# Feed-forward products on two halves of the array, own block per iteration, and small reciprocals, in a fused attention and feed-forward kernel

## The reference

```python
xn = _layernorm(x)
q, k, v = xn @ wq + bq, xn @ wk + bk, xn @ wv + bv      # 16 query heads, 2 key/value heads of 16
q, k = rotated(q) * hd ** (-0.5), rotated(k)            # sin/cos tables over the 1024 positions
attn = softmax(einsum('bqhd,bkhd->bhqk', q, k_exp) * hd ** (-0.5))
a = einsum('bhqk,bkhd->bqhd', attn, v_exp).reshape(b, s, d) @ wo + bo
hidden = fwht(silu(xn @ W1.T) * (xn @ W3.T))            # 1024 wide, Walsh-Hadamard transform
out = x + a + hidden @ W2.T
```

## Time and profile before

| | us |
|---|---|
| median of 3 runs | 1303.58 |
| lowest and highest | 1293.02, 1316.16 |
| the profiled execution | 1307.79 |
| its span, first to last instruction | 1305.6 |
| mean granted clock of TensorE | 0.904 of 2.4 GHz |
| busy: PE, DVE, ACT, POOL | 1125.1, 827.6, 711.4, 351.6 |

### The profile page before, as it was taken

One profiled execution on the slowest core, in us unless ns is written; L12 is line 12 of the kernel. 1 busy time (PEld: TensorE's weight loads), 2 busy tenths in 40 slices (PEclk: granted clock), 3 DMA queues, 4 the chain that ended last, 5 costly groups with the idle time before them and its releaser, 6 DMA issues.

```text
span 1305.6 us, 16047 instructions
## 1 busy us (share of the span) xinstructions
PE 1125.1 (86%) x6048; PEld 538.3 (41%) x6048; DVE 827.6 (63%) x860; ACT 711.4 (54%) x1320; POOL 351.6 (27%) x300
## 2 busy tenths in 40 slices
PE   2276899978998899988998899978998999998985
PEld 1243454543444444443444434444444344533322
DVE  3766547666676657667676767667766667656611
ACT  2123347654674557654774557655774467544561
POOL 1836503205241053305241053105330013100000
PEclk9698899988998989999998999989999699977675
DMA  6330012000120022100120022000200011000001
GB/s 201 102 106 1 3 62 84 22 20 20 54 76 22 23 93 69 36 19 23 56 73 21 24 94 84 21 22 25 70 22 26 10 41 46 21 21 9 9 9 41
DMA packets 44796, 58.08 MB, mean 44 GB/s; under 512 B 11184, under 2 KB 26416, under 8 KB 44720
## 3 DMA queue, kind: packets, MB, share of 16 engines
q1 hardware_dynamic: 41408, 52.34, 13.7%
q10 hardware_dynamic: 3312, 4.72, 1.0%
HBM read 33.95 MB, written 13.63 MB: 36 GB/s over the span
## 4 chain that ended last, share of the span: by engine, by line
PE 73%; DVE 15%; issue 6%; POOL 2%; ACT 2%; ACTq 1%; SPq 0%; DMA 0%; POOLq 0%
PE ps L963 27%; PE ps L983 14%; PE ps L1067 14%; PE ps L1054 14%; DVE negpart L832 8%; PE ps L993 3%; DVE recips L863 2%; DVE y L869 1%; DVE y L814 1%; DVE stats L788 1%; PE ps L999 1%; DVE mturned L858 1%; ACTq L648 1%; DVE xnt L799 1%; DVE mturned L856 1%
## 5 line engine op out<-in xcount | busy, mean ns | idle before, releaser
L832 DVE TENSOR_REDUCE negpart<-ps 128x2 f32<-128x1024 f32 x512 | 626.5, 1225 | 388.8 <-PE ps L983 388.1
L709 ACT ACTIVATE work<-ps 128x512 f32<-128x512 f32 x1024 | 553.2, 598 | 396.1 <-PE ps L1054 391.0
L983 PE MATMUL ps<-kb,qh 48*128 48x512 f32 x1024 | 253.6, 480 | 106.5 <-DVE negpart L832 28.7
L1067 PE MATMUL ps<-work,vb 128*32 128x512 f32 x2048 | 301.3, 663 | 1.3 <-ACT work L709 1.2
L1054 PE MATMUL ps<-qh,kb 50*128 50x512 f32 x1024 | 271.9, 493 | 11.2 <-ACT work L709 11.2
L983 PEld LDWEIGHTS ps<-kb,qh 48*128 48x128 f32 x1024 | 105.8, 199 | 323.9 <-issue 139.7
L963 PE MATMUL ps<-xnt,w_p 128*128 128x512 f32 x768 | 218.4, 421 | 10.5 <-DVE negpart L832 6.5
L1054 PEld LDWEIGHTS ps<-qh,kb 50*128 50x128 f32 x1024 | 112.1, 200 | 147.5 <-issue 67.8
L963 PEld LDWEIGHTS ps<-xnt,w_p 128*128 128x128 f32 x768 | 138.3, 193 | 82.6 <-issue 49.9
L585 POOL TENSOR_TENSOR hid_p<-hid,hid_p 128x512 fp32r<-128x512 f32 x64 | 83.3, 1302 | 203.0 <-ACT hid_p L700 203.0
L581 POOL TENSOR_TENSOR hid<-hid 128x512 f32<-128x512 f32 x64 | 82.3, 1286 | 188.4 <-ACT hid L696 188.4
(11 more groups left out here) (104 smaller groups left out, 458.4 us busy)
## 6 DMA issues: line engine op xcount, KB each, us to landing
qh<-qk_parts SPq DMA_DIRECT2D x192, 64.0 KB, 2.1
y<-in_x SPq DMA_DIRECT2D x8, 512.0 KB, 4.2
recips<-osum SPq DMA_DIRECT2D x128, 32.0 KB, 2.0
attnt<-osum SPq DMA_DIRECT2D x128, 32.0 KB, 2.0
out<-y SPq DMA_DIRECT2D x8, 512.0 KB, 2.8
xn<-in_x SPq DMA_DIRECT2D x7, 512.0 KB, 3.9
qk_parts<-qe SPq DMA_DIRECT2D x14, 256.0 KB, 2.4
qk_parts<-xn SPq DMA_DIRECT2D x14, 256.0 KB, 2.4
```

Source lines behind the costliest of these rows:

```text
L709: nc.scalar.activation(prob[j % 2][:, h, :], ps[:, 4 + u % 3, :], ACT.Exp, scale=SCALE).then_inc(exp_done, 1)
L832: nc.vector.tensor_reduce(negpart[a][:, f, :, h, t, e], two(slot), AX.X, ALU.max, negate=True).then_inc(ring_free[slot], 1)
L983: m = pe.matmul(bank[:, r, :], qh[2 * q + f][rows, h, t * P:(t + 1) * P], kb[i % 2][rows, e * 512:(e + 1) * 512], start=True, stop=True)
L1067: m = pe.matmul(ps[VW * h:VW * (h + 1), 7, :], vb[b % 2][g][:, kt, :], prob[j % 2][:, h, :], start=(kt == 0), stop=(kt == ST - 1))
```

## The change

- UP: rows 0 to 63 of the array hold `W1`'s weights and rows 64 to 127 `W3`'s. The 256 input rows are taken in four parts of 64 (`KC`), so a chunk has 24 matmuls of 64 rows, in 12 pairs that write two banks. The tokens have to stand in both halves of the partitions: SP writes the turned tokens (`xt`) to DRAM (`store_turned`) and reads them back twice (`load_turned`) into `xf`.
- DN: 48 matmuls of 64 rows, in 24 pairs; each half sums into a bank of its own, and VectorE adds both (`down`).
- UP and DN of block i stand in iteration i, for all 8 iterations. In the opening stand 24 S1 alone.
- The row of tokens gives way to an order for each kind of period. A kind with `x` is one in which an MT or a VT stands too. ScalarE's and VectorE's orders have kinds too.
- The reciprocals are taken of one copy of each sum, 128 x 32 numbers, through DRAM (`turn_sums`, `spread_recips`), and spread to 128 x 512 by eight transfers.
- The statistics of block i + 3 are taken at p = 8 to 12, one tile each, not together after p = 13, and its normalisation at p = 13 and 14.
- `mturned` has one buffer for each half instead of two; `recips` one instead of two.

```diff
@@ main_entry @@
-        return ("WO", i - 1, p - 2) if i > 0 else ("DN", 0, p - 2)
-    if 4 <= p < 12 and i + 1 < NBLK:
-        return ("UP", i + 1, p - 4)
-    if p >= 12 and i + 1 < NBLK:
-        return ("DN", i + 1, p - 12)
+        return ("WO", i - 1, p - 2) if i > 0 else ("W2", p - 2)
+    if 4 <= p < 12:
+        return ("UP", i, p - 4)
+    if p >= 12:
+        return ("DN", i, p - 12)
@@ walk_iteration @@
+        if kind == "UP":
+            own(0, 1)
+            first(1)
+            scores(0)
+            extra()
+            sums_before()
+            scores(1)
+            first(1)
+            own(2, 3)
+            first(1)
+            scores(2)
+            sums(i, 2 * p)
+            scores(3)
+            first(1)
...
+        elif kind == "XT":
+            sums_before()
+            own(0)
+            first(1)
+            extra()
+            first(1)
+            scores(0)
+            own(1)
+            scores(1)
...
@@ move_sums, on SP @@
-                for h in range(QUAD):
-                    to = (a * QUAD + h) * HD
-                    sp.dma_start(recips[to:to + HD, f, :], osum[VW * h + HD:VW * (h + 1), :]).then_inc(moved[f], 16)
+                sp.dma_start(sums_rows[f, a * QUAD:(a + 1) * QUAD, :], osum[HD:P:VW, :]).then_inc(sums_out[f], 16)
...
+            def turn_sums(i, f):
+                sp.wait_ge(sums_out[f], 32 * (i + 1))
...
+                sp.dma_start(dens[f][:, :], sums_rows[f].rearrange("h (g n) -> (h g) n", g=HD)).then_inc(dens_in[f], 16)
+
+            def spread_recips(i, f):
+                sp.wait_ge(recip_done[f], i + 1)
...
+                sp.dma_start(recip_rows[f].rearrange("h (g n) -> (h g) n", g=HD), dens[f][:, :]).then_inc(recip_out[f], 16)
+                sp.wait_ge(recip_out[f], 16 * (i + 1))
+                for h in range(2 * QUAD):
+                    sp.dma_start(recips[HD * h:HD * (h + 1), :],
+                                 recip_rows[f, h].partition_broadcast(HD)).then_inc(recips_in, 16)
@@ down and reciprocals, on VectorE @@
-                nc.vector.tensor_tensor(at, at, two(slot)[:, 0, 0:D], ALU.add).then_inc(ring_free[slot], 1)
+                nc.vector.tensor_tensor(at, at, two(slot)[:, 0, 0:D], ALU.add).then_inc(down_half, 1)
+                dve.wait_ge(down_half, BT * m + t + 1)
+                nc.vector.tensor_tensor(at, at, two(slot)[:, 1, 0:D], ALU.add).then_inc(ring_free[slot], 1)
...
-                dve.wait_ge(moved[f], N_MOVE * 2 * (i + 1))
-                nc.vector.reciprocal(recips[:, f, :], recips[:, f, :]).then_inc(recip_done, 1)
+                dve.wait_ge(dens_in[f], 16 * (i + 1))
+                nc.vector.reciprocal(dens[f][:, :], dens[f][:, :]).then_inc(recip_done[f], 1)
@@ UP on TensorE (DN alike, with 256 columns) @@
-                    m = product(bank[:, k // 2, :], [v[:, kk, c * P:(c + 1) * P] for v in w],
-                                [v[:, kk, :] for v in xnt[n % 2]], kk == 0, kk == 1)
+                    for t, (w, v) in enumerate(TERMS):
+                        for r in range(ROWT):
+                            rows = slice(GRP * r, GRP * (r + 1))
+                            m = pe.matmul(bank[:, r, :], w13_p[w][rows, k, c * P:(c + 1) * P], xf[v][rows, k, :],
+                                          start=(k == 0 and t == 0), stop=(done and t == 2))
```

665 lines of the change are left out of this document (462 added, 203 removed).

## The result

The changed kernel took 1180.56 us in the median of four runs (1178.65 to 1181.6), the kernel before, measured beside it, 1308.87 (1293.02 to 1316.16). The ratio is 0.9091, with a 95% interval of 0.9025 to 0.9158: 9.1% faster.

The account below looks back on a forecast made before the run. TensorE was taken to bound the up periods, the down periods partly something else. Gains of 22.5 + 30.3 + 57.5 + 13.4 + 9.3 - 4 = 129.0 us from 1307.8 gave 1179 us, range 1130 to 1240.

Parts of the forecast that it names:

- The stretches of one shape: TensorE: every stretch of one array shape costs about 0.2 us on top of 0.233 per 512 columns.
- Rival 1: Half-array pairs don't hide their weight loads: pairs of about 0.33 us, up period 8.8, 1323 us in all; 7%.
- Up, 61.2 forecast: p = 4 to 11: loop of 7.4 us through slot 0, held until `gated` read it; 61.2 for 65.6, gain 4.4 per iteration.
- Down, 33.2 forecast: p = 12 to 15: 33.2 us for 41.0, with small reciprocal and spread statistics; gain 7.8 per iteration, between 4 and 9.
- p = 0 to 3, put at 39.0: First four periods of an iteration: 39.0 us for 38.7, no gain, ends -5 and +4.
- The wait for ScalarE's copies: p = 0: transposes' copy precedes the exponentials, TensorE waits at the second score; 2.5 us lost.
- Iteration 0, 137.4 forecast: First iteration: 39.0 + 4 for a cold start + 61.2 + 33.2 = 137.4 us against 167.7, gain 30.3.
- Iterations 6 and 7, 130.4 and 119.2 forecast: Last two iterations: 130.4 us for 143.8, gain 13.4, and 119.2 for 128.5, gain 9.3.
- Opening 95 for 96: Before iteration 0's first score: 96 us for 118.5, as up product 0 goes away; gain 22.5.
- end 24.6 for 26.4: Kernel's end: the last 3.34 us reciprocal goes, a longer chain of some 7.4 us comes; loss 4.
- Rival 3: WO at p = 3 or ring slots wait 4 us more per iteration, or up periods stay near 7.9: 1210 us; 20%.
- Rival 2: Half-array products don't lift TensorE's clock from 0.50: some 5 us more per period, 1419 us with half of them; 6%.

Follow-up runs that it names:

- the old order with halves: Both feed-forward products in half-array pairs, in the kernel before, order and reciprocals untouched: 1337.14 us, ratio 1.0168.
- the three parts alone: Kernel before with only halves (ratio 1.0168), only small reciprocals (0.9876), or only the rest: orders, own block, tokens through DRAM, spread statistics (1.0148).

## Why the prediction was right

**The stretches of one shape: right.** Pairs of 0.232 and 0.118 are the medians over all up and down periods; six pairs of UP took 1.5 for the 1.4 forecast (587.45 to 588.95, 591.08 to 592.57), since in either a wait for a slot stands at one end. Rival 1 is out: its 0.34 occurs only at the first pair of a stretch or behind such a wait. The Trainium skill's rule ("TensorE: Matmul & The Clock Gate", section "The mechanism") that a weight load overlaps a running matmul only when their row groups differ, would by itself have made each pair wait for its weights, since neighbouring pairs use the same row groups; this trace speaks against it, with those same 0.232 us. The first paragraph of the same section also lets a load go ahead when it targets a background weight buffer, and with that the trace agrees; no run here tests it by itself.

**Up, 61.2 forecast, 60.8 measured.** The loop from the first up pair of a plain period to that of the next is 7.53 for 7.4 (579.92 to 587.45), with the two stretches of six pairs 0.1 longer each. The bound is the one named, the slot until `gated` has read it: the pair of 587.45 starts as `gated` ends, 0.41 behind the S1 before it where 0.23 would do, so the wait itself is 0.18. By first exponentials p = 4 to 7 took 30.95 and p = 8 to 11 29.9, for 30.6 each: the closeness of the sum is in part two misses of opposite sign. What the step left unsaid is that the gate has to wait for the whole product now. It counted the loop of the new order only; the old order with halves shows what that costs where nothing covers it, 0.65 a period.

**Down, 33.2 forecast.** p = 12 and 13 took 8.09 and 7.98 for 8.0, p = 14 8.85 for 8.7, and p = 15 8.4 for 8.5 in iterations 5 and 6, where no transposes follow it. The statistics and the reciprocal are gone from p = 14 (14.9 before), and the experiments put 5.0 on the reciprocal in the old kernel and 4.1 to 5.4 in the new, the low clock behind the stall included, which the step didn't have; the statistics, with 1.1 left between 9.9 and 8.85, were not tried alone. The reciprocal takes 0.34 for 0.3.

**p = 0 to 3, put at 39.0 where the kernel before had 38.7.** With p = 12 to 15 it was to be 72.2 and is 72.9 in iteration 3. The wait for ScalarE's copies is where it was put, at 2.5 us; without it p = 15 and 0 together are 3.2 shorter. What the step didn't have is the clock: p = 0 runs at the low level in all of iterations 1 to 5. In iterations 1 and 3 that ends soon after p = 1 begins, which takes 10.5 and 10.25; in 2, 4 and 5 it lasts 13.7 us and p = 1 takes 12.7 to 12.9. The rows are, for iteration 3, the low stretch and what follows it, and for iteration 4 the low stretch, which goes through p = 0 and half of p = 1:

```profile
516.80:523.60 6.80, 5.84 (x23) 3.13 (x24) 3.56 (x4) 4.81 (x10) 0.00 (x0) 0.50 0.41 149
523.60:533.40 9.80, 9.70 (x50) 4.85 (x48) 5.14 (x6) 5.75 (x12) 0.00 (x0) 1.00 0.08 23
649.90:663.50 13.60, 12.08 (x41) 5.93 (x42) 7.17 (x6) 7.68 (x15) 0.00 (x0) 0.50 0.25 89
```

The mean of iterations 1 to 5 is 135.3 for 133.4. The three long falls make some 7 of the 9.4 us that the five iterations are over the forecast, the largest miss of the sum.

**Iteration 0, 137.4 forecast, 145.4 measured.** The term `39.0 + 4 for a cold start` was too small: by first exponentials p = 3 alone took 17, with W2's transform (eight full-array matmuls, 2.02 us), projections, and a clock at 0.70. Eight matmuls of the transform, and the first up product behind a wait of 1.3:

```profile
134.39 2.02 PE L1359 MATMUL ps<-y,osum 128*128 128x256 f32 x8
...
142.53 2.93 PE L1339 MATMUL ps<-xf,w_p 64*128 64x512 f32 x12 [1.32 <-DVE negpart L1124]
```

The same 12 matmuls take 1.56 at full clock.

**Iterations 6 and 7, 130.4 and 119.2 forecast, 124.6 and 113.8 measured.** Periods 0 and 1 were put at 8.5 each, from the low clock of the earlier trace rows; the row of 917.00 above shows them at full clock, 5.6 each. The difference, 17.0 for 11.25, is 5.75, and the two iterations missed by 5.8 and 5.4. That iteration 7's feed-forward work would be cheap was right (11 us for all of it).

**Opening 95 for 96; end 24.6 for 26.4.** The row of the opening ends where the transposes of p = 0 begin. The first score, which the forecast counted to and which now stands behind them, comes at 98.3; counted that way the opening missed by 2.3 and iteration 0 by 4.7. The end's chain is as counted, with eight issues of 0.47 each where 0.6 was taken:

```profile
1162.60 0.35 DVE L1157 RECIPROCAL dens<-dens 128x32 f32<-128x32 f32 x1 [2.57 <-DMA dens<-sums_rows]
1162.98 0.34 SPq L712 DMA_DIRECT2D recip_rows<-dens  x1
1164.42 3.77 SPq L715 DMA_DIRECT2D recips<-recip_rows  x8
...
1169.87 1.26 POOL L831 TENSOR_TENSOR attnt<-attnt,recips 128x512 f32<-128x512 f32 x1 [18.69 <-DMA recips<-recip_rows]
1171.28 3.75 PE L1307 MATMUL ps<-wo_sb,attnt 128*128 128x256 f32 x8 [12.51 <-POOL attnt L831]
```

**Rival 3 (late chains): out.** TensorE waits for GpSimd's `attnt` once in the kernel, at the end, and the up loop is 7.53, not 7.9. Its waits by releaser (us in total, times, longest):

```profile
PE ps L1297 <- DVE negpart L1124: 27.4, 42, 3.9
...
PE ps L1307 <- POOL attnt L831: 12.5, 1, 12.5
```

**Rival 2 (clock): out as put.** With half-array products the clock is at 1.00 through p = 4 to 11 of iterations 1 to 7. Its lesson stays, though: the large misses were mostly the clock's: +8 in iteration 0 in part, +9.4 in 1 to 5, -5.8 and -5.4 in 6 and 7. With -1.0 at the opening and -1.8 at the end they cancelled to some 3 us in the profiled execution and 1.6 in the median, which is luck; a total so close says little of its terms.

What stays open: why the low level at p = 0 lasts 6.8 us in two iterations and 13.7 in three with the same instructions (p = 1 takes 10.25, 10.53, 12.72, 12.86, 12.88 in one execution). No run separates that. Where the low level begins stand, in each of the five, the same two waits of TensorE, 1.3 for a maximum and the 1.67 shown above; they don't tell the long falls from the short ones.

## What to carry to other kernels

Count stretches of one array shape, not only matmuls: here every stretch costs about 0.2 us, and products in the shape of their neighbours don't pay it again. But when two products that ended one after the other end together, whoever reads the first starts later; look for what is queued behind that reader, since half-array products were 1.7% slower in the old order and 5% faster in the changed kernel. When an edit's parts are measured one by one, measure the corners too: here the three parts alone gave between 1.7 points lost and 1.2 won, and 9.1 won together.
